# Reciprocals and inverse roots by exp of a scaled log and one Newton step

## What is computed

```python
# layer 0
logits = einsum('bhqd,bhkd->bhqk', x @ Wq, ctx @ Wk) * 64 ** -0.5 + col_bias
x = einsum('bhqk,bhkd->bhqd', softmax(logits), ctx @ Wv) @ Wo + bo + x
# layers 1 to 3
inv = rsqrt(mean(x * x, -1) + 1e-5)
q = (x * inv * norm_w) @ wq
attn = softmax(einsum('btgrd,bsgd->bgrts', q, ctx @ wk) / sqrt(32))
x = x + einsum('bgrts,bsgd->btgrd', attn, ctx @ wv) @ wo
```

## Time and profile before

| | us |
|---|---|
| median of 3 runs | 4727.58 (4726.94 to 4730.17) |
| profiled execution, its span | 4730.0 |
| context projections | 0 to 1041 |
| layer 0, one iteration of 8 | about 170 |
| layers 1 to 3, one iteration of 24 | 92.95 |

### The profile page before, as it was taken

How to read it: one execution, slowest core, us unless ns; L and a number is a source line. 1 busy time by engine, 2 the same in 40 slices (tenths; PEclk the granted TensorE clock), 3 DMA queues, 4 the chain that set the end, 5 groups by cost and what they waited for, 6 DMA issues and landing times. The chain is left out here.

```text
span 4730.0 us, 63902 instructions
## 1 busy us (share of the span) xinstructions
PE 4434.4 (94%) x20450; PEld 2718.5 (57%) x20450; DVE 2572.9 (54%) x3575; ACT 1926.9 (41%) x2348; POOL 1579.5 (33%) x827
## 2 busy tenths in 40 slices
PE   7999799978999999999969999999999999999998
PEld 6888688864555655565535454445444544454454
DVE  2211200015455455544557767776777677767776
ACT  2111211113333333333326555655565555555554
POOL 0000000002444435434424444444444443444444
PEclk9999899998999999999979999999999999999999
DMA  4333422234434444444432232232222222222233
GB/s 158 127 129 133 148 83 82 80 99 120 115 100 118 115 108 111 118 107 113 113 89 71 82 88 71 75 98 83 73 74 86 84 82 75 84 85 73 75 89 95
DMA packets 301727, 461.94 MB, mean 98 GB/s; under 512 B 44954, under 2 KB 95130, under 8 KB 301692
## 3 DMA queue, kind: packets, MB, share of 16 engines
q1 hardware_dynamic: 301692, 461.50, 33.6%
HBM read 227.88 MB, written 102.76 MB: 70 GB/s over the span
## 5 line engine op out<-in xcount | busy, mean ns | idle before, releaser
L803 DVE TENSOR_REDUCE a_max_cols<-a_ps 128x1 f32<-128x512 f32 x2072 | 1343.8, 680 | 422.7 <-PE a_ps L930 419.3
L699 ACT ACTIVATE a_probs<-a_ps 128x1024 f32<-128x1024 f32 x1024 | 1018.6, 1026 | 730.7 <-PE a_ps L951 727.1
L930 PE MATMUL a_ps<-a_k_ops,a_q_ops 96*128 96x512 f32 (+1 forms) x2592 | 957.9, 435 | 71.9 <-DVE a_max_cols L803 50.8
L930 PEld LDWEIGHTS a_ps<-a_k_ops,a_q_ops 96*128 96x128 f32 (+1 forms) x2592 | 459.4, 190 | 696.2 <-DVE a_max_cols L803 547.3
L951 PE MATMUL a_ps<-a_q_ops,a_k_ops 128*128 128x512 f32 x2560 | 785.2, 409 | 37.7 <-ACT a_probs L699 19.1
L823 DVE RECIPROCAL a_stage<-a_ps 128x128 f32<-128x128 f32 x640 | 571.6, 928 | 396.1 <-PE a_ps L979 396.0
L593 POOL TENSOR_TENSOR a_probs<-a_probs 128x1024 f32<-128x1024 f32 x192 | 462.6, 2409 | 729.7 <-PE a_ps L967 708.5
L967 PE MATMUL a_ps<-a_probs,a_v 128*32 128x512 f32 (+1 forms) x4096 | 677.2, 612 | 0.0
L668 ACT ACTIVATE a_q_ops<-a_ps 1x512 fp32r<-1x512 f32 x518 | 304.9, 589 | 781.7 <-PE a_ps L938 777.3
L951 PEld LDWEIGHTS a_ps<-a_q_ops,a_k_ops 128*128 128x128 f32 x2560 | 463.9, 190 | 206.8 <-ACT a_probs L699 82.7
L599 POOL TENSOR_TENSOR a_qn_lo<-a_qf,a_qn_hi 128x512 fp32r<-128x512 f32 x99 | 126.5, 1278 | 1040.9 <-ACT a_qn_hi L660 1040.9
(11 more groups left out here) (88 smaller groups left out, 5315.9 us busy)
## 6 DMA issues: line engine op xcount, KB each, us to landing
a_k_ops<-k_scratch SPq DMA_DIRECT2D x201, 256.0 KB, 3.9
a_q_ops<-a_qn_hi SPq DMA_DIRECT2D x792, 64.0 KB, 2.0
k_scratch<-kp_out SPq DMA_DIRECT2D x88, 512.0 KB, 2.8
a_q_ops<-a_qn_hi SPq DMA_DIRECT2D x268, 128.0 KB, 2.3
a_x_raw<-out_t SPq DMA_DIRECT2D x26, 1024.0 KB, 5.2
a_q_ops<-a_qn_lo SPq DMA_DIRECT2D x396, 64.0 KB, 2.0
a_x_res<-out_t SPq DMA_DIRECT2D x96, 256.0 KB, 3.1
out_t<-a_results SPq DMA_DIRECT2D x96, 256.0 KB, 2.0
```

The costliest lines, as they stand in the source:

```text
L699: act.activation(probs[:, s], ps[:, 2 * (s % 2):2 * (s % 2) + 2, :], ACT.Exp)\
L803: dve.tensor_reduce(max_cols[:, col:col + 1], bank(MAXB[n]), AX.X, ALU.max, negate=True).then_inc(reduced, 1)
L930: last = pe.matmul(bank(MAXB[n]), q_ops[0:rows(p), s, h, p, q * P:(q + 1) * P], k_ops[0:rows(p), s, k_head(h), p, :], start=(p == 0), stop ...
```

## The change

A reciprocal of a denominator d becomes: ScalarE's natural log of d (`log_denominators`), its exp of minus that (`guess_reciprocals`), a first guess g in `guess`; then three VectorE instructions (`divide`): d g, (d g - 2) g, and that times -1 times the output, which is one Newton step and the normalising multiply. The inverse root becomes a log, an exp of -0.5 times it and three VectorE instructions with the scale folded in (`invert_mean_square`). All run over 512 columns at once. The three instructions of a division stand after reductions 0, 1 and 2 of the next tile, those of the inverse root after reductions 4, 5 and 6 of tile 1. The first of a division reads PSUM and SBUF, the second two SBUF tensors, the third SBUF and PSUM; the three of the inverse root read two SBUF tensors each. One set of ScalarE's function tables, with log and exp, is loaded ahead of each loop. The last line of the diff makes room for the two new SBUF tensors. New semaphores are left out.

```diff
+    DIVIDE_AT = (0, 1, 2)
...
-    PARTS, EARLY = 4, (3 if has_norm else 2)
...
+        guess = sb("guess", [P, S], F32)
+        step_of = sb("step_of", [P, S], F32)
...
-            def inv_rms(n):
-
-                act.wait_ge(ms_step, MS * (n + 1))
-                act.activation(inv[:, :], ms[:, 1, :], ACT.Sqrt, scale=scale * scale).then_inc(inv_done, 1)
+            def log_mean_square(n):
+                act.wait_ge(ms_mean, n + 1)
+                act.activation(ms[:, 1, :], ms[:, 0, :], ACT.Ln).then_inc(ms_log, 1)
+
+            def guess_inv_rms(n):
+
+                act.wait_ge(ms_log, n + 1)
+                act.activation(ms[:, 1, :], ms[:, 1, :], ACT.Exp, scale=-0.5).then_inc(ms_guess, 1)
+
+            def log_denominators(it, t):
+                act.wait_ge(den_done, it * T + t + 1)
+
+                act.wait_ge(normed, 1 + it * T + t)
+                act.activation(guess[:, :], bank(DENB), ACT.Ln).then_inc(den_log, 1)
+
+            def guess_reciprocals(it, t):
+
+                act.wait_ge(den_log, it * T + t + 1)
+                act.activation(guess[:, :], guess[:, :], ACT.Exp, scale=-1.0).then_inc(den_guess, 1)
...
+            act.preload_act_table_set("natural_log_exp_and_others")
...
-                inv_rms(0)
+                log_mean_square(0)
+                guess_inv_rms(0)
...
                             round_x(it + 1, 0 if has_norm else s // 2)
                         if has_norm and t == T - 1 and s == NS - 1:
                             squares(it + 2)
-                        if has_norm and t == 1 and s == NS - 1:
-                            act.wait_ge(q_taken, (it + 1) * T)
-                            inv_rms(it + 1)
+                        if has_norm and t == 0 and s == NS - 1:
+                            log_mean_square(it + 1)
+                        if has_norm and t == 1 and s == 0:
+                            guess_inv_rms(it + 1)
...
-                    shift(*place(it, t + 1))
-                    if not has_norm:
+                    if has_norm:
+                        log_denominators(it, t)
+                        if t == T - 1:
+                            guess_reciprocals(it, t)
+                        shift(*place(it, t + 1))
+                        if t < T - 1:
+                            guess_reciprocals(it, t)
+                    else:
+                        shift(*place(it, t + 1))
+                        log_denominators(it, t)
+                        if t == T - 1:
+                            guess_reciprocals(it, t)
                         round_q(*place(it, t + AHEAD))
+                        if t < T - 1:
+                            guess_reciprocals(it, t)
...
             def invert_mean_square(n, i):
 
-                w = S // PARTS
                 if i == 0:
-                    dve.wait_ge(ms_step, MS * n + 1)
-                dve.reciprocal(ms[:, 1, i * w:(i + 1) * w], ms[:, 0, i * w:(i + 1) * w]).then_inc(ms_step, 1)
+                    dve.wait_ge(ms_guess, n + 1)
+                    dve.tensor_tensor(ms[:, 0, :], ms[:, 0, :], ms[:, 1, :], ALU.mult).then_inc(ms_step, 1)
+                elif i == 1:
+                    dve.wait_ge(ms_step, 2 * n + 1)
+                    dve.scalar_tensor_tensor(out=ms[:, 0, :], in0=ms[:, 0, :], scalar=-0.5 * scale, in1=ms[:, 1, :],
+                                             op0=ALU.mult, op1=ALU.mult).then_inc(ms_step, 1)
+                else:
+                    dve.wait_ge(ms_step, 2 * n + 2)
+                    dve.scalar_tensor_tensor(out=inv[:, :], in0=ms[:, 0, :], scalar=1.5 * scale, in1=ms[:, 1, :],
+                                             op0=ALU.add, op1=ALU.mult).then_inc(inv_done, 1)
...
-            def reciprocals(it, t, parts):
-
-                n = S // PARTS
-                for i in parts:
-                    if i == 0:
-                        dve.wait_ge(den_done, it * T + t + 1)
-                        if not has_norm and t < 2:
-                            dve.wait_ge(stored[t], 1 + it * (2 * DMA))
-
-                        if t >= 2:
-                            dve.wait_ge(o_lo, it * T + t - 1)
-                    dve.reciprocal(stage[:, t % 2, i * n:(i + 1) * n], bank(DENB)[:, i * n:(i + 1) * n])\
-                        .then_inc(recip_done, 1)
-
-            def normalise(it, t):
-                dve.wait_ge(recip_done, (it * T + t + 1) * PARTS)
-                dve.tensor_tensor(stage[:, t % 2, :], bank(OUTB), stage[:, t % 2, :], ALU.mult).then_inc(normed, 1)
+            def divide(it, t, i):
+
+                if i == 0:
+                    dve.wait_ge(den_guess, it * T + t + 1)
+                    dve.tensor_tensor(step_of[:, :], bank(DENB), guess[:, :], ALU.mult).then_inc(div_step, 1)
+                elif i == 1:
+                    dve.wait_ge(div_step, 2 * (it * T + t) + 1)
+                    dve.scalar_tensor_tensor(out=step_of[:, :], in0=step_of[:, :], scalar=-2.0, in1=guess[:, :],
+                                             op0=ALU.add, op1=ALU.mult).then_inc(div_step, 1)
+                else:
+                    dve.wait_ge(div_step, 2 * (it * T + t) + 2)
+                    dve.wait_ge(pv, 1 + (it * T + t + 1) * KT)
+                    if not has_norm and t < 2:
+                        dve.wait_ge(stored[t], 1 + it * (2 * DMA))
+                    if t >= 2:
+                        dve.wait_ge(o_lo, it * T + t - 1)
+                    dve.scalar_tensor_tensor(out=stage[:, t % 2, :], in0=step_of[:, :], scalar=-1.0, in1=bank(OUTB),
+                                             op0=ALU.mult, op1=ALU.mult).then_inc(normed, 1)
...
-                        if has_norm and t == 0 and n == NS + PARTS:
-                            invert_mean_square(it + 1, 0)
-                        if has_norm and t == 0 and n == M - 1:
-                            invert_mean_square(it + 1, 1)
-                            invert_mean_square(it + 1, 2)
-                        if has_norm and t == 1 and n == NS:
-                            invert_mean_square(it + 1, 3)
-
-                        if t > 0 and n == 0:
-                            if not has_norm:
-                                reciprocals(it, t - 1, range(PARTS - 1, PARTS))
-                            else:
-                                normalise(it, t - 1)
-                        if t > 0 and n == 1 and not has_norm:
-                            normalise(it, t - 1)
+                        if has_norm and t == 1 and n in (4, 5, 6):
+                            invert_mean_square(it + 1, n - 4)
+                        if t > 0 and n in DIVIDE_AT:
+                            divide(it, t - 1, DIVIDE_AT.index(n))
...
-                    reciprocals(it, t, range(EARLY))
                     take_q(*place(it, t + AHEAD))
-                    if t < T - 1:
-                        reciprocals(it, t, range(EARLY, PARTS - 1 + LATE))
-                    else:
-                        reciprocals(it, t, range(EARLY, PARTS))
-                        normalise(it, t)
+                    if t == T - 1:
+                        for i in range(3):
+                            divide(it, t, i)
...
+    nc = bacc.Bacc("TRN2", target_bir_lowering=False, num_devices=1, dynamic_dma_scratch_size=1024)
```

17 lines of the change are left out of this document (10 added, 7 removed).

## The result

| | before | after |
|---|---|---|
| median, us | 4727.75 (4726.94 to 4730.17, 4 runs) | 4961.72 (4957.0 to 4972.75, 4 runs) |
| ratio | | 1.0497 (1.0482 to 1.0512) |
| profiled span, us | 4730.0 | 4954.9 |
| mean granted clock of TensorE | 0.977 | 0.963 |
| VectorE busy, us | 2572.9 | 2308.5 |

The change makes the kernel 5.0% slower. It was forecast 4915 us, 4.0% slower; the time lies inside the range of 4770 to 4985, 47 us above the forecast.

A forecast was written before the change was run, and what follows sets the result against it. TensorE, busy 97% of each stretch, was taken as the bound. Terms of 7.45 us in each of 24 iterations (179) plus 8 for layer 0 gave +187 on 4727.58, hence 4915 us; range 4770 to 4985.

The forecast's parts named there:

- The lock of VectorE and GpSimd: Tile 1, layers 1 to 3: inverse-root steps take turns with GpSimd's additions, waiting whole instructions; +4.6 us an iteration.
- GpSimd first: Rival, tiles 2 and 3: GpSimd's subtraction starts before the second division step; +1.3 us each, 4977 us; chance 0.20 with clock.
- The start of a tile: Layers 1 to 3: division chain ends late, maxima 4 go 1.1 us late; +0.9 a tile, +0.85 in tile 2.
- The clock: Tile 1, layers 1 to 3: TensorE's clock falls behind its waits for the inverse-root steps; +1.5 us an iteration.
- a rival, which gave it 1 us in all 72 tiles: Wait ahead of maxima 4 lowers the clock in tiles 1 to 3; 4987 us; chance 0.20 shared with GpSimd first.
- Tile 0 and the end of the iteration: Layers 1 to 3: a reciprocal goes in tile 0, −0.8 us; later shift and chained division steps at the end, +0.4.
- Layer 0: 56 tiles: the same division chain lets the outputs go later; +0.15 us a tile, 8 us in all.
- Table loads: ScalarE: loads nearly all in idle time; the one leaving tile 2 had held it by 0.05 us at most.
- chain: Tile starts in layers 1 to 3: three division steps interleaved with three reductions; +0.9 us a tile, +0.85 in tile 2.

The follow-up runs named there:

- `root_idle_reduces`: `root_idle` plus three unused VectorE reductions, one SBUF input each, behind reductions 4, 5 and 6 of tile 1: 4853.3 us.
- `root_idle`: Kernel after, inverse root moved to idle places: log, exp and first two steps at the end of tile 0, third step late in tile 1: 4851.31 us.
- `div_early`: `root_idle` with the whole division at each tile's end in layers 1 to 3, log and exp ahead of the shift: 4747.77 us.
- `old_div`: Kernel after with the division as before (four reciprocals and a multiply), the inverse root still new: 4859.76 us, ratio 1.0281.
- `old_div_norm3`: `old_div_root_idle` with the normalising multiply behind reduction 3 instead of reduction 0 in layers 1 to 3: 4796.55 us.
- `old_root`: Kernel after with the inverse root as before (reciprocals and ScalarE's square root), the division still new: 4882.56 us, ratio 1.0324.
- `old_div_root_idle`: `root_idle` with the division as before, so only the inverse root is new, in idle places: 4697.83 us, ratio 0.9930.
- `root_idle_011`: `root_idle` with the second and third division steps both behind reduction 1, in layer 0 too: 4785.15 us.
- `root_idle_000`: `root_idle` with all three division steps behind reduction 0: 4886.48 us.

## Why the prediction was right, and where it was off

**The lock of VectorE and GpSimd: right, and the largest term.** Forecast were steps of 1.9, 2.2 and 2.3 us by one meeting in the earlier trace rows; measured 1.65, 2.28 and 2.23 (medians 1.65, 2.27, 2.23). The additions of 2.8 us in tile 1 are there, 2.79 at 2705.35. The Trainium skill ("SBUF — State Buffer", Who interferes with whom) says that a VectorE instruction with two SBUF inputs and a GpSimd one that reads SBUF exclude each other, and that reductions take no part. Both agree with this case: 2.28 us for a step, 0.677 for a reduction in the same place (`root_idle_reduces`). Tile 1 as a whole: 6.1 forecast, 5.97 in an ordinary iteration (26.10 less 20.13). Part of this closeness is luck. By the earlier trace rows the first addition ends at 2583.12 + 2.37 + 0.15 = 2585.6, not at the 2586.3 that the working used, which would have made the term 0.65 smaller. And the working had no term for ScalarE's exp for the root in tile 1. With it `qn_lo` starts 0.57 us later in the tile than before (7.01 us against 6.44 behind its start) and GpSimd's additions 0.55 later, not 0.15; where that exp stands elsewhere (`root_idle`), `qn_lo` starts at 6.48. The two errors nearly cancel. On the scores that exp costs nothing here, since the wait ahead of maxima 4 is shorter by as much, 0.95 instead of 1.29. The mean is only 5.26, because in every eighth iteration the tile took 25.4 to 26.9 us before as well, and the change adds 0.3 to 1.8 there: these tiles wait and run at a lower clock already before the change. Why so little is added there wasn't tried. The sum had priced these three iterations like the rest, 14 us too much.

**GpSimd first: fell.** The second step of the division never came second. It takes 0.68 in the median and 0.693 at most over all 160. In tiles 2 and 3 it is a matter of 0.03 to 0.05 us, not of the 0.17 forecast, and GpSimd pays:

```profile
2724.88 0.68 DVE L865 SCALAR_TENSOR_TENSOR a_step_of<-a_step_of,a_guess 128x512 f32<-128x512 f32 x1
2724.92 1.76 POOL L607 TENSOR_TENSOR a_qn_lo<-a_qf,a_qn_hi 128x512 fp32r<-128x512 f32 x1 [15.11 <-ACT a_qn_hi L683]
```

1.76 instead of the 1.28 of the earlier trace rows. The instruction that starts first keeps its time, as the rule in that rival has it.

**The start of a tile: right mechanism, 0.3 us too small.** The step that failed is the spacing. It was taken from the earlier trace rows as 0.54 behind a reduction and 0.59 behind a multiply; in a chain that alternates, all stand at 0.60. Maxima 4 went 4.17 behind maxima 0, not 3.95. That is +1.33 over the earlier trace rows where +1.1 was forecast, and of the 0.2 that was to come back behind it next to nothing did: tiles 3 at full clock are 1.28 longer, tiles 2 1.18. The mis-sized term is worth ((1.28 − 0.9) + (1.18 − 0.85)) × 24 = 17 us.

**The clock: one place named, three there are.** The 1.5 us of tile 1 was right in size: 0.59 over the 4 us from 2709 loses 1.6, and the two tiles 1 without such a fall behind their waits took 24.6 us instead of 26.1. But the sum gave nothing to tiles 2 and 3, where the wait ahead of maxima 4 is 1.3 us; that was left to a rival, which gave it 1 us in all 72 tiles. Measured: 22 of 48 tiles 2 and 3 have it, 12 + 6 of 1.5 us and 4 of 2.9, 38 us. This is the largest error of the sum. That the wait is its cause shows in `div_early` and `old_div`, in which tiles 2 and 3 have neither the wait nor a second value, and in `old_div_norm3`, where the wait comes back alone and 14 of 72 tiles have one. (In the kernel after, the clock falls behind maxima 4 in 8 tiles 1 as well; their length does not show it.)

**Tile 0 and the end of the iteration: −0.15 instead of −0.4.** `old_div` and `old_root` take the two apart. The reciprocal of the earlier trace rows that goes is worth 0.79 (33.38 to 32.59; forecast 0.8). The end of the iteration costs 0.64 (33.38 to 34.02), the upper bound of the 0 to 0.65 that had been given, not 0.4. 6 us.

**Layer 0: forecast +8, measured +4.6, by luck.** A tile is 0.38 longer, above the upper bound of 0.35: 48 × 0.38 = 18. The forecast chain ends at 1324.7, 4.35 us behind maxima 0, where its own spacing of 0.54 and 0.59 gives 1324.5; in the kernel after it takes 4.5. Against it stands tile 6 of an iteration, in which TensorE waits for x before and after: 21.49 on average before, 19.88 after. That term was in no step of the prediction. Most of it is the clock. Before, it falls behind that wait in seven of the eight tiles 6; after, the wait is 0.5 us shorter and the clock falls in one. The tiles 6 without a fall take 19.9 before and 19.7 after. The same tile before and after, the wait and 4 us behind it (columns as above):

```profile
1208.11 0.80 PE L915 MATMUL a_ps<-a_x_hi,a_wq_hi 128*128 128x512 f32 x1 [2.83 <-DVE a_x_lo L809]
1208.00:1212.00 4.00, 3.89 (x11) 2.85 (x13) 0.05 (x1) 0.00 (x0) 1.19 (x1) 0.58 0.00 0
```

```profile
1209.37 0.50 PE L948 MATMUL a_ps<-a_x_hi,a_wq_hi 128*128 128x512 f32 x1 [2.30 <-DVE a_x_lo L855]
1209.00:1213.00 4.00, 3.63 (x14) 2.11 (x15) 0.32 (x1) 0.21 (x1) 1.46 (x1) 1.00 0.01 1
```

That the shorter wait is why the clock holds was not tried.

**Table loads: right at nothing.** The earlier trace rows had 48 ahead of exps, and there were 25 more at the square root; now two are left in the layers, one ahead of each loop:

```profile
L700 ACT ACT_TABLE_LOAD x2 | 2.6, 1283 | 28.0 <-PEq L263 25.4 <-PEq L51 2.5
```

The tally against the forecast of +187: chain +17, clock in tiles 2 and 3 +38, end of the iteration +6, three iterations at a change of layer −14, layer 0 −3, together +231; measured are +225 on the span. The other −6 lie in tile 1, in the two tiles without a fall of the clock and in 0.13 us of each other one. The median lies another 7 us above the profiled execution.

## What to carry to other kernels

An instruction that replaces another in an engine's list has to be priced by its place, not by its duration: the same three steps of the inverse root cost TensorE nothing in gaps and 7.4 us a tile 1 beside GpSimd's additions, a fall of the clock included (19.55 in `old_div_root_idle`, 27.0 in `old_div`), and 264 us less work for VectorE did not make up for it. Before a long reciprocal is split into dependent short steps, count the instructions of the engine between the data and the one that waits for it; six at 0.60 us were 1.3 us later than two. And the best version (4697.8 us) came from taking the change apart: its half with slack all around it, the root, gained, its half with a deadline, the division, lost in all four places where it was put, 50 us in the best (4697.8 to 4747.8).

## What the runs showed of the hardware

A wait of 1.3 us of TensorE can cost 1.5 us more behind it, in a clock of 0.50 for about 3 us. It comes in some tiles and not in others of one execution, and the wait's length alone doesn't order them: of the 72 tiles 1 to 3, 8 had it behind waits of 0.92 us, all in tiles 1 and 2, none behind the 0.99 of tile 3 (`root_idle_011`), 14 behind 1.38 (`old_div_norm3`), 26 behind 1.29 (`root_idle`), 35 behind 1.45 to 1.53 (`root_idle_000`). The short wait in `root_idle_011` came with the fewest falls and the longest one with the most. What decides between two tiles with the same instructions and the same wait, as at 2726.81 and 3247.06, stays open.

Where VectorE and GpSimd exclude each other, they alternate: in all 72 meetings in tile 1 of the kernel after, VectorE's step ended 0.55 us behind the end of an addition, and the addition that followed the first and second step took 2.79 to 2.86 instead of 2.39. A waiting VectorE instruction is shown as a long one, not as idle time, so it is found by its duration in the groups by line (2205 ns against 683 for the same form), never among the waits.
